# Each of GpSimd's two-operand operations on 512 columns written as two of 256

## What is computed

```
# layer 0 (W1a, W1b: the halves of W1)
mask = adj > 0
h    = relu((x @ W1a)[:, :, None] + (x[:, :, None] - x[:, None, :]) @ W1b + b1)
hm   = einsum('bjkh,bjk->bjh', h, mask)
x    = layernorm(x + hm @ W2 + mask.sum(-1) * b2)
# layer 1: a message by the weighted edges, and a GRU cell
m    = relu(relu(x @ W1 + b1) @ W2 + b2)
msg  = relu(einsum('bij,bjh->bih', adj, m))
r, z = sigmoid(i_r + h_r), sigmoid(i_z + h_z)
n    = tanh(i_n + r * h_n)
x    = layernorm(x + (1 - z) * n + z * x)
```

## Time and profile before

| | us |
|---|---|
| median of 3 runs | 804.74 |
| the profiled execution | 805.59 |
| its span, first to last instruction | 804.1 |
| TensorE busy | 695.8 (87%) |
| VectorE busy | 762.4 (95%) |
| ScalarE busy | 640.9 (80%) |
| GpSimd busy | 549.3 (68%) |

### The profile page before, as it was taken

How to read it: one execution, slowest core, us unless ns; L and a number is a source line. 1 busy time by engine, 2 the same in 40 slices (tenths; PEclk the granted TensorE clock), 3 DMA queues, 4 the chain that set the end, 5 groups by cost and what they waited for, 6 DMA issues and landing times.

```text
span 804.1 us, 37406 instructions
## 1 busy us (share of the span) xinstructions
PE 695.8 (87%) x15984; PEld 568.7 (71%) x15984; DVE 762.4 (95%) x851; ACT 640.9 (80%) x1897; POOL 549.3 (68%) x625
## 2 busy tenths in 40 slices
PE   3768789889898989989899898989989898988885
PEld 2547677677787867768787777878677687867662
DVE  5799999999999999999999999999999999998983
ACT  5746676888888888888988888888988888887654
POOL 5534445677868677786867779696777969575772
PEclk9999999999999999999999999999999999999998
DMA  5533243233334323323323232433223243222000
GB/s 150 146 105 75 83 100 88 62 75 101 75 100 97 86 76 75 104 73 108 95 81 84 66 113 63 121 81 94 75 65 111 68 120 76 56 61 75 2 15 27
DMA packets 33316, 66.86 MB, mean 83 GB/s; under 512 B 5504, under 2 KB 6272, under 8 KB 33152
## 3 DMA queue, kind: packets, MB, share of 16 engines
q1 hardware_dynamic: 33152, 64.48, 30.3%
HBM read 22.52 MB, written 4.19 MB: 33 GB/s over the span
## 4 chain that ended last, share of the span: by engine, by line
issue 44%; PE 28%; DVE 21%; ACT 3%; DMA 2%; POOL 1%; SPq 0%; DVEq 0%; POOLq 0%
PE PS L649 20%; DVE AC L1196 11%; DVE AC L1217 7%; PE PS L903 3%; PE PS L968 2%; PE PS L723 2%; PE PS L886 1%; DMA VA<-VN 1%; DVE WM L1165 1%; ACT VN L1565 1%; DMA bs<-in_rows 1%; POOL MT L1780 0%; DVE AC L1212 0%; DVE DM L1175 0%; ACT YO L1484 0%
## 5 line engine op out<-in xcount | busy, mean ns | idle before, releaser
L1217 DVE SCALAR_TENSOR_TENSOR AC<-PS,AC 128x1152 f32<-128x1152 f32 (+4 forms) x288 | 333.2, 1157 | 11.6 <-PE PS L649 10.7
L1196 DVE SCALAR_TENSOR_TENSOR AC<-PS,AC 128x1152 f32<-128x1152 f32 (+4 forms) x256 | 291.0, 1137 | 1.6 <-PE PS L903 1.3
L649 PE MATMUL PS<-DM,VA 128*64 128x192 fp8e5 (+1 forms) x2048 | 126.4, 244 | 41.4 <-DVE AC L1196 29.5
L649 PEld LDWEIGHTS PS<-DM,VA 128*64 128x64 f16 x2048 | 81.3, 110 | 77.8 <-DVE AC L1196 49.6
L649 PE MATMUL PS<-DM,VB 128*64 128x192 fp8e5 (+1 forms) x2048 | 123.9, 240 | 0.7 <-DVE AC L1212 0.2
L903 PE MATMUL PS<-DM,VB 128*64 128x192 fp8e5 (+1 forms) x1024 | 85.9, 245 | 23.7 <-DVE AC L1217 19.2
L1175 DVE TENSOR_SCALAR DM<-CW 128x1536 uint16<-128x1536 uint16 (+1 forms) x132 | 96.2, 750 | 1.0 <-DMA CW<-WM 1.0
L649 PEld LDWEIGHTS PS<-DM,VB 128*64 128x64 f16 x2048 | 89.5, 110 | 2.6 <-DVE AC L1217 1.5
L1812 POOL TENSOR_TENSOR XE<-XQ,XT 128x512 f16<-128x512 f32 x32 | 41.3, 1289 | 70.2 <-ACT XT L1552 70.2
L1838 POOL TENSOR_TENSOR AC<-AC,SD 128x512 f32<-128x512 f32 (+1 forms) x62 | 65.3, 1063 | 29.4 <-DVE DM L1175 29.4
L903 PEld LDWEIGHTS PS<-DM,VB 128*64 128x64 f16 x1024 | 45.6, 108 | 54.1 <-DVE AC L1217 26.9
(11 more groups left out here) (240 smaller groups left out, 2067.5 us busy)
## 6 DMA issues: line engine op xcount, KB each, us to landing
CW<-WM SPq DMA_DIRECT2D x128, 160.0 KB, 2.8
XQ<-in_xq SPq DMA_DIRECT2D x32, 256.0 KB, 2.7
VA<-VN SPq DMA_DIRECT2D x64, 128.0 KB, 2.3
VB<-VN SPq DMA_DIRECT2D x64, 128.0 KB, 2.3
AT<-in_adjt SPq DMA_DIRECT2D x15, 512.0 KB, 4.6
XN<-in_xn SPq DMA_DIRECT2D x16, 256.0 KB, 4.4
out<-YO SPq DMA_DIRECT2D x15, 256.0 KB, 2.1
WG<-in_wg SPq DMA_DIRECT2D x1, 515.5 KB, 7.5
```

The costliest lines, as they stand in the source:

```text
L649: last = e.matmul(o[k], lhs[:, k], rhs, **flags)
L1196: e.scalar_tensor_tensor(t, tiles(PS[:, b + p:b + 3, :])[:, :, cols], 0.0, t, ALU.max, ALU.add).then_inc(s["sx"], 1)
L1217: e.scalar_tensor_tensor(t, tiles(PS[:, r, :])[:, :, cols], 0.0, t, ALU.max, ALU.add).then_inc(s["sy"], 1)
```

## The change

A helper `in_two` gives a function `twice`, which issues an operation on the first half of the second dimension and then on the second half; only the second half tells a semaphore. Fourteen calls of `e.tensor_tensor` in GpSimd's stages go through it. Waits, data, results and the lists of the other engines stay as they are.

```diff
+        def in_two(e):
+
+            def twice(o, x, y, op):
+                n = o.shape[1] // 2
+                e.tensor_tensor(o[:, 0:n], x[:, 0:n], y[:, 0:n], op)
+                return e.tensor_tensor(o[:, n:], x[:, n:], y[:, n:], op)
+
+            return twice
         def gpsimd_layer1(e, po, s):
+            twice = in_two(e)
...
             def gd(u):
                 if late(u):
                     return
                 po.wait_ge(s["tanh"], u + 1)
-                e.tensor_tensor(GT[:], XGf[u % 2], GN[:], ALU.subtract).then_inc(s["gd"], 1)
+                twice(GT[:], XGf[u % 2], GN[:], ALU.subtract).then_inc(s["gd"], 1)
                 po.wait_ge(s["gd"], 3 * u + 1)
                 po.wait_ge(s["sig"], 2 * u + 2)
-                e.tensor_tensor(GT[:], GT[:], GZ[:], ALU.mult).then_inc(s["gd"], 1)
+                twice(GT[:], GT[:], GZ[:], ALU.mult).then_inc(s["gd"], 1)
...
             def split_h(u):
                 po.wait_ge(s["hh"], u + 1)
                 po.wait_ge(s["yt"], 2 * u)
-                e.tensor_tensor(GTl[:], GT[:], SYf, ALU.subtract).then_inc(s["hl"], 1)
+                twice(GTl[:], GT[:], SYf, ALU.subtract).then_inc(s["hl"], 1)
...
             def x_split(q):
                 po.wait_ge(s["xqh"], q + 1)
                 po.wait_ge(s["o0"], q - 3)
-                e.tensor_tensor(XE[q % 4][:, :, nat], XQ[:], XT0[:], ALU.subtract).then_inc(s["xql"], 1)
+                twice(XE[q % 4][:, :, nat], XQ[:], XT0[:], ALU.subtract).then_inc(s["xql"], 1)
...
                 po.wait_ge(s["ini"], 2 * q + k + 1)
-                e.tensor_tensor(u, u, NNB[:, 4 * k:4 + 2 * k, :], ALU.mult).then_inc(s["im"], 1)
+                twice(u, u, NNB[:, 4 * k:4 + 2 * k, :], ALU.mult).then_inc(s["im"], 1)
...
-                    e.tensor_tensor(t[:, h, nat], t[:, h, nat], SD[q % 3][:, h, :], ALU.add).then_inc(s["ad"], 1)
+                    twice(t[:, h, nat], t[:, h, nat], SD[q % 3][:, h, :], ALU.add).then_inc(s["ad"], 1)
```

More of the change, by code:

```diff
@@ L1721, in gt @@
                 po.wait_ge(s["sig"], 2 * u + 1)
-                e.tensor_tensor(GT[:], GT[:], GR[:], ALU.mult).then_inc(s["gt"], 1)
+                twice(GT[:], GT[:], GR[:], ALU.mult).then_inc(s["gt"], 1)
             def gt_in(u, b, gates):
@@ L1728, in gt_in @@
                 po.wait_ge(s["gt"], 2 * u + 1)
-                e.tensor_tensor(GT[:], GT[:], M1f, ALU.add).then_inc(s["gt"], 1)
+                twice(GT[:], GT[:], M1f, ALU.add).then_inc(s["gt"], 1)
             def gd(u):
@@ L1743, in h @@
                 po.wait_ge(s["gd"], 3 * u + 2)
-                e.tensor_tensor(GT[:], GT[:], GN[:], ALU.add).then_inc(s["gd"], 1)
+                twice(GT[:], GT[:], GN[:], ALU.add).then_inc(s["gd"], 1)
                 po.wait_ge(s["gd"], 3 * u + 3)
-                e.tensor_tensor(GT[:], GT[:], XGf[u % 2], ALU.add).then_inc(s["h"], 1)
+                twice(GT[:], GT[:], XGf[u % 2], ALU.add).then_inc(s["h"], 1)
             return {"power1": power1, "gt": gt, "gt_in": gt_in, "gd": gd, "h": h, "power2": power2}
         def gpsimd_main(e):
-            po, s = Lane(e), main
+            po, s, twice = Lane(e), main, in_two(e)
             def setup():
@@ L1785, in split_xg @@
                     po.wait_ge(s["gate"], 4 * u)
-                    e.tensor_tensor(XGl[:], XGf[u % 2], XGh[:], ALU.subtract).then_inc(s["xgl"], 1)
+                    twice(XGl[:], XGf[u % 2], XGh[:], ALU.subtract).then_inc(s["xgl"], 1)
             def split_x1(u):
@@ L1791, in split_x1 @@
                     po.wait_ge(s["xg"], u)
-                    e.tensor_tensor(X1l[:], X1[:], SQ[:], ALU.subtract).then_inc(s["x1l"], 1)
+                    twice(X1l[:], X1[:], SQ[:], ALU.subtract).then_inc(s["x1l"], 1)
             def split_h(u):
@@ L1802, in split_ms @@
                     po.wait_ge(s["gate"], 4 * u)
-                    e.tensor_tensor(MSl[:], MSf, MSh[:], ALU.subtract).then_inc(s["ml"], 1)
+                    twice(MSl[:], MSf, MSh[:], ALU.subtract).then_inc(s["ml"], 1)
             def split_x(g):
                 po.wait_ge(s["xh"], g + 1)
-                e.tensor_tensor(XHL[g % 2][:, :, 1, :], XN[:], XHL[g % 2][:, :, 0, :], ALU.subtract).then_inc(s["xl"], 1)
+                twice(XHL[g % 2][:, :, 1, :], XN[:], XHL[g % 2][:, :, 0, :], ALU.subtract).then_inc(s["xl"], 1)
             def x_split(q):
```

## The result

The changed kernel took 822.75 us in the median of four runs (822.0 to 823.33), beside 804.63 (804.32 to 805.43, four runs) for the kernel before: ratio 1.022, 95% interval 1.0205 to 1.0234, slower. The forecast was 821.5. The profiled execution has a span of 820.5, 16.4 more than before; the medians differ by 18.1.

A forecast was written before the change was run, and what follows sets the result against it. VectorE, 95% busy, was taken as the bound, with GpSimd as full in one stretch of each period. Twelve periods x 1.3 = 15.6, plus 0.4 and 0.7 outside, gave +16.7: 821.5 us; range 812 to 826 (8 in 10).

The forecast's parts named there:

- The price of a split: On GpSimd, each operation issued in halves was to cost 0.15 us more; bounds 0 and 0.17.
- rival B: Splits nearly free on GpSimd: 801 us with 0 each, 801 to 808 with 0 to 0.05 each; chance 0.07.
- VectorE's savings: Three VectorE instructions per period held less at the port shared with GpSimd: 0.52, 0.27 and 0.2, together 0.97 us.
- Rival E: At the port a second half passes the waiting DM, nothing saved at 388.91: 819 to 824; chance inside the forecast's 0.82.
- The pair at 367.88: Two VectorE word generations (DM): first ends 0.49 earlier, GpSimd's second half precedes the second; saved 0.0, at most 0.49.
- Rival D: The second DM at 367.88 goes before GpSimd's second half: 5.9 us less, 815.6; chance inside the forecast's 0.82.
- The chain: GpSimd's eleven split instructions from 388.03 to L1797's end: 1.65 for splits plus 0.13, so L1797 ends 1.78 us later.
- yt: TensorE's step that needs L1797: slack 0.43, so it starts 1.35 us later; VectorE's L1196 behind it 0.9 late.
- L1715 and L1155: Later in the period: GpSimd's L1715 1.35 late; through ScalarE, VectorE's L1155 (slack 0.05) is 1.3 us late.
- Rival C: If L1155 has more slack, only the yt stall counts: 0.9 a period, 816.6; chance inside the forecast's 0.82.
- Rival A: The chain up to L1797 has room, so VectorE keeps 0.97 x 12 = 11.6 us: 794; chance 0.08.
- The sum: Whole kernel: 12 periods x 1.3 = 15.6, plus 0.4 outside them and 0.7 in the tail: +16.7 us.

The follow-up runs named there:

- the control: The kernel before, all operations whole, with the period's 512-column scale_u moved behind the layer norm's power (power2): 812.42 us, ratio 1.0086.

## Why the prediction was right, by its steps

The total was right to 1.25 us and the mechanism is the one forecast: GpSimd's longer chain makes yt late, then the power, and VectorE waits behind both. But the sum came out through errors in both directions.

- **The price of a split** was put at 0.15. The two halves of L1744 take 401.53 to 402.95, 1.42, where the whole took 1.27: 0.15. On 128 columns, cut from 256: 400.70 to 401.57, 0.87 against 0.73, 0.14. Both lie within the bounds, 0 and 0.17; rival B, nearly free splits, is out.
- **VectorE's savings: the step that failed.** 0.97 were credited (its own three terms, 0.52, 0.27 and 0.2, add up to 0.99). The rows show 0.35, and by that the instruction ahead of the yt step's L1196 ends earlier, at 16.94 instead of 17.29. The DM of 388.91 fell to 0.55 as foretold, and its 0.52 went into L1217's idle, 0.32 to 0.84. The step took a shorter instruction on VectorE for a gain without asking what the next one waits for: TensorE's batch, which starts on L1196. The DM of 391.57 thus came at 3.53 as before, not 0.52 earlier, and took 1.08, not 0.92. L1165 took 1.02 (1.07 foretold), held by the second half of L1744 and not by its first. Saved: 0.11 and 0.24. Rival E, with nothing saved at 388.91, is out as well.
- **The pair at 367.88:** foretold as unchanged, because the blocked second half goes ahead of the second DM. 1.98 for the pair, 1.97 to 1.99 before. Rival D is out.
- **The chain.** L1797 was to end 1.78 later, and ended 1.52 later. The port's share was foretold as 1.47; read it is 0.25 and 0.34 at `gd`, 0.31 at AC, and 0.47 at the first half of L1746, where 0.57 was said of the second half of L1744: 1.37, 0.03 over the 1.34 before. So 1.49 is left for eleven splits, 0.135 each.
- **yt** was to start 1.35 late. The earlier trace rows put it 15.25 after `gd`, now it is at 16.37: 1.12. The slack was 0.40 and not 0.43. The batch behind it was to be as late as yt, but is 0.88 late (16.08 before, 16.96 now): yt to batch took 0.83 and takes 0.59. From its load to L1196 it was to need 0.7, a term that no row showed; it is 0.78 now (411.24 to 412.02), and before there was slack in it. VectorE's L1196 is 0.52 late, not 0.9. The idle time of 0.79 ahead of it is that 0.52 and the 0.35 by which VectorE was early, less the 0.07 by which the two instructions overlapped before.
- **L1715 and L1155.** The power ends 1.14 late (1.35 foretold), SI starts at 24.67 instead of 23.55: 1.12 (1.3 foretold). The period grew by 1.21, and the last 0.09 was left out of the sum: the nine other splits of the period were said to be swallowed by GpSimd's waits, but the second half of `scale_u` at 441.15 holds the DM ahead of the next `gd` (0.63 for 0.55). Rival C, only yt's stall, is out: VectorE is 0.52 late behind yt and 1.12 late at SI. Rival A needed the chain to have room, and it had 0.40.
- **The sum.** 12 x 1.21 = 14.5 where 15.6 stood. Outside of the periods 16.4 - 14.5 = 1.9 where 0.4 + 0.7 stood; 0.2 of it lies ahead of the first `gd` and 1.7 behind the twelfth period, which I haven't followed. The two errors, -1.1 and +0.8, nearly cancel, and that is luck. The low end of the range, 812, was said to be C and D together; at their own prices, 4.8 and 5.9, they give 810.8.
- **The busy times:** VectorE down 6.2, foretold 10 to 14. That rested on 0.97 less in each of twelve periods, 11.6. The DM of 391.57 accounts for 1.9 of what is missing. The sums of L1196 and L1217 take 2.2 more in all (626.4 for 624.2), and the eight DMs on 768 columns, outside of the periods, 0.9 more (3.7 for 2.8). VectorE's idle time was to grow by over 25, and grew by (820.5 - 756.2) - (804.1 - 762.4) = 22.6. GpSimd is up by 53, foretold 49.

The failed step did not move the total much for a reason that the prediction gives itself: whatever VectorE wins ahead of a GpSimd chain that is already late is waited away at yt. Had the chain had 2 us of slack, the same error would have been worth 12 x 0.62 = 7.4, by my estimate from these rows.

The Trainium skill, "SBUF — State Buffer", section "Who interferes with whom", has it that issue order decides who blocks. The runs agree at each meeting of a DM with a sum, product or difference of GpSimd's read here, but not at the power in the kernel with `scale_u` behind `split_h`: it had started 1.50 ahead of the DM, and it was the one that got longer (2.08 for 1.67). That shorter GpSimd instructions would free VectorE holds for the instruction (1.07 to 0.55). For the time it gave nothing at the DM of 388.91, nothing on top of L1165 at that of 391.57, and 0.28 a period at L1165.

## What to carry to other kernels

An engine whose busy share over the span leaves room (68% here) can be full in the one stretch that a consumer waits behind; count the added instructions in that stretch, times the price of one, against the slack of the next consumer in its fixed order, and then of the one behind that. A shorter instruction on the bound engine is a gain only if nothing else ends the next instruction's wait; look at who released it. Split only where a held instruction is followed at once by work that was waiting for it alone: one such place was worth 0.4%, all of them together cost 2.2%.

## What the runs showed of the hardware that was not expected

- Moving an operation by less than 0.3 us can cost as much: the same DM behind a whole L1838 took 1.19, 1.47 and 1.61 where L1838 started 3.03, 3.31 and 3.46 after `gd`. It took 0.64 to 1.08 where L1838 was in halves.
- GpSimd's power instruction on 8 columns took 1.64 to 1.68 in every kernel, but 2.08 or 2.09 twelve times in the one with `scale_u` behind `split_h`, where a DM falls into it, though it has hardly any data; the DM took its 0.55, as if alone.
- The prediction had one case, at 38.15, for a blocked GpSimd instruction that goes ahead of a second VectorE instruction. Now it stands in each period: 1.03 for each of the two DMs, where the first had taken 1.50 and the second 0.55.
- In most kernels one or two periods of the profiled execution, between 340 and 440 us, were longer (46.72 for 46.58 before, 48.98 for 47.18 in the control). The cause stays open; none of them is a period whose rows are laid side by side here.
